# A GRU scan with a mixture of experts on one core: the order of TensorE's products by stationary width, and the update gate's place in PSUM

## What is computed

```
for each step:  gi = x_t @ W_ih + b_ih ;  gh = h @ W_hh + b_hh          # 512 -> 3*512
                r, z = sigmoid(i_r + h_r), sigmoid(i_z + h_z)
                n = tanh(i_n + r * h_n) ;  h = (1 - z) * n + z * h
tokens = all h:  logits = tokens/|tokens| @ router_w  -> softmax, top 2 of 8, renormalised
out = x + sum_e combine[:, e] * (tokens @ Wa[e] @ Wb[e])                 # 512 -> 128 -> 512
```

## Time and profile before

| what | value |
| --- | --- |
| time, median of 3 runs | 1042.74 us (1042.63 to 1043.17) |
| the profiled execution | 1042.57 us |
| its span | 1040.8 us |
| busy: TensorE, its weight loads, VectorE, ScalarE, GpSimd | 97%, 80%, 83%, 69%, 29% |
| mean granted clock of TensorE | 0.998 |

### The profile page before, as it was taken

How to read it: one execution, slowest core, us unless ns; L and a number is a source line. 1 busy time by engine, 2 the same in 40 slices (tenths; PEclk the granted TensorE clock), 3 DMA queues, 4 the chain that set the end, 5 groups by cost and what they waited for, 6 DMA issues and landing times.

```text
span 1040.8 us, 67010 instructions
## 1 busy us (share of the span) xinstructions
PE 1011.4 (97%) x28409; PEld 828.4 (80%) x28409; DVE 860.0 (83%) x3215; ACT 722.6 (69%) x2824; POOL 299.0 (29%) x762
## 2 busy tenths in 40 slices
PE   5789999999999999999999999999999999999997
PEld 3677888888888888888888888888888888888875
DVE  6889888888888888888888888888888888888886
ACT  7687666767666767667767667667766767766663
POOL 2032232322233332233332233332233332223223
PEclk9999999999999999999999999999999999999999
DMA  8230111111111111111111111111111011110001
GB/s 295 84 94 17 30 32 29 30 27 30 29 32 29 29 27 30 29 32 30 29 28 28 29 32 32 27 30 27 29 32 32 26 30 28 29 32 20 9 9 33
DMA packets 49522, 39.24 MB, mean 38 GB/s; under 512 B 34676, under 2 KB 39112, under 8 KB 49224
## 3 DMA queue, kind: packets, MB, share of 16 engines
q1 hardware_dynamic: 48376, 31.41, 11.1%
q10 hardware_dynamic: 848, 3.54, 1.0%
HBM read 18.94 MB, written 8.39 MB: 26 GB/s over the span
## 4 chain that ended last, share of the span: by engine, by line
PE 91%; DVE 5%; ACT 2%; DMA 1%; issue 1%; POOL 0%; ACTq 0%; DVEq 0%; POOLq 0%
PE ybank L1014 18%; PE pairs L883 17%; PE obank L1037 15%; PE gates L958 11%; PE gates L963 10%; PE nbank L912 7%; PE zbank L973 5%; PE zbank L969 5%; DVE tr L762 1%; PE nbank L994 1%; DMA wih<-in_L_cond_W_ih 1%; DVE pre L765 1%; DVE acc L815 1%; ACT nn L624 1%; DVE pre L771 1%
## 5 line engine op out<-in xcount | busy, mean ns | idle before, releaser
L883 PEld LDWEIGHTS pairs<-wx,xs 128*32 128x32 f16 x6144 | 140.7, 96 | 105.8 <-issue 101.7
L883 PE MATMUL pairs<-wx,xs 128*32 128x256 f16 x6144 | 215.6, 275 | 0.0
L1014 PE MATMUL ybank<-hparts,wa 128*128 128x128 f16 x3024 | 212.5, 220 | 0.0
L458 POOL TENSOR_TENSOR y<-y 128x128 f16<-128x128 f32 x256 | 111.7, 436 | 348.1 <-ACT y L658 190.0
L1037 PE MATMUL obank<-wb,y 128*128 128x512 f16 x738 | 199.3, 379 | 0.0
L1014 PEld LDWEIGHTS ybank<-hparts,wa 128*128 128x128 f16 x3024 | 169.8, 98 | 26.9
L762 DVE STREAM_TRANSPOSE tr<-gates 128x256 f32<-128x256 f32 x256 | 115.1, 450 | 72.4 <-PE gates L963 68.5
L616 ACT ACTIVATE rr<-pre 128x64 f32<-128x64 f32 x256 | 65.7, 257 | 155.6 <-DVE pre L765 155.2
L958 PE MATMUL gates<-whh,st 128*32 128x256 f16 x4080 | 155.8, 273 | 11.3 <-DVE st L788 10.8
L963 PE MATMUL gates<-whh,hparts 128*32 128x256 f16 x4080 | 155.9, 273 | 0.0
L815 DVE SCALAR_TENSOR_TENSOR acc<-obank,comb,acc 128x512 f32<-128x512 f32 x184 | 136.9, 744 | 0.2
(11 more groups left out here) (134 smaller groups left out, 1701.4 us busy)
## 6 DMA issues: line engine op xcount, KB each, us to landing
out<-outb SPq DMA_DIRECT2D x63, 128.0 KB
xin<-in_x SPq DMA_DIRECT2D x58, 128.0 KB
wih<-in_L_cond_W_ih ACTq DMA_DIRECT2D x4, 768.0 KB, 7.7
whh<-in_L_cond_W_hh SPq DMA_DIRECT2D x4, 768.0 KB, 11.8
wih<-in_L_ffn_Wb SPq DMA_DIRECT2D x8, 256.0 KB, 2.7
xs<-xh SPq DMA_TRANSPOSE x116, 2.8
wih<-in_L_ffn_Wa SPq DMA_DIRECT2D x4, 256.0 KB, 4.2
whh<-in_L_ffn_Wa SPq DMA_DIRECT2D x4, 256.0 KB, 2.6
```

Of the source, the lines that this page charges most:

```text
L458: nc.gpsimd.tensor_tensor(y[:, m % YB, 1, :], y32[:, :], y[:, m % YB, 0, :], ALU.subtract).then_inc(ylo_ready, 1)
L883: mm = nc.tensor.matmul(bank[32 * j:32 * j + 32, P:3 * P], turned(b, k, ph)[:, t0:t0 + 2 * B], wx[:, pw, k, j, :], start=False, stop=(k == ...
L1014: mm = nc.tensor.matmul(y_at(m)[:, 0:P], wa[:, pw, k, e, :], hparts[:, f % HB, k, :, ph * B:(ph + 1) * B], start=(n == 0), stop=(n == 3 * ...
```

## The change

Steps are now of two kinds. An odd step, behind its `state_part`, does only products with 128 stationary columns: the last term of the second expert's `expert_up`, an `expert_down`, all 12 products of an `n_part`, the route at s = 3, and a second `expert_down`. An even step does only products with 32 stationary columns, and it does a whole `pair_part` (48 products) and then five of the six terms of two experts' `expert_up`. A term there is four products in the four column groups, each with 32 of the 128 stationary columns and all 512 moving ones.

For that PSUM is dealt out anew. `zbank` is gone: the update gate of step n is in columns 256 to 383 of `gates[(n + 1) % 2]`, the bank in which the next step's other gates are made, so the products of the update gate also wait until `seed(n + 1)` is done. There are two output banks (`obanks`). The experts' middle is in `ybank` for even experts and beside the candidate's part in `nbank` for odd ones; the router's sums are beside it in `ybank`. On ScalarE `seed` now stands ahead of the router's copy and `split_y`. The expert work runs one step later (`DOWN`, `SPLIT` = 9, `ADD` = 14), so that 14 outputs, and not 13, are left behind the last step.

```
-    DOWN, UP, ADD = S, S + 5, S + 5
-    YB = UP - DOWN + 1
-    AHEAD = 3
+    DOWN, SPLIT, ADD = S + 1, S + 1, S + 6
+    YB = 6
...
-        zbank = ps("zbank", [P, 4 * P])
-        obank = ps("obank", [P, 4 * P])
+        obanks = [ps(f"obank{i}", [P, 4 * P]) for i in range(2)]
+        def z_at(n):
+            return gates[(n + 1) % 2][:, 2 * P:3 * P]
         def y_at(m):
+            return nbank[:, 2 * P:3 * P] if m % 2 else ybank[:, 0:P]
+        def router_at(f):
+            return (ybank if f < NB - 1 else gates[1])[:, P:P + NE + 1]
...
             def seed(n):
                 wait(act, rh_turned, n - 1)
+                wait(act, z_turned, n - 2)
...
             def add_gi_bias(b, m):
                 act.wait_ge(gi_done, K * b + m + 1)
-                if b >= 2 and m == 1:
-                    act.wait_ge(logits_done, b - 1)
+                if b >= 2:
+                    act.wait_ge(y_done, (b - 2) * NE + 2 * m + 2)
...
             def beside(n):                              # ScalarE
+                if n + 2 < T:
+                    seed(n + 2)
                 if s == 3 and 1 <= i:
                     read_router(i - 1)
-                if 0 <= n - DOWN:
-                    split_y(n - DOWN)
-                if n + 2 < T:
-                    seed(n + 2)
+                if 0 <= n - SPLIT:
+                    split_y(n - SPLIT)
...
                 mm.then_inc(rh_done, 1)
                 pe.wait_ge(z_seeded, n + 1)
+                pe.wait_ge(seeded, min(n + 2, T))
...
             def expert_down(m):
+                wait(pe, yhi_ready, m - 1)
+                wait(pe, y32_ready, m - 1)
+                if m % 2 == 0 and e >= NE // 2 and m < LAST:
+                    pe.wait_ge(router_read, f + 1)
+                if m % 2:
+                    pe.wait_ge(gi_ready, min(K * (f + 2) + m % NE // 2, K * NB))
...
+            def up_term(m, term, tiles):
+                ph, pw = TERMS[term]
+                rows = P // tiles
+                for j in range(tiles):
+                    mm = nc.tensor.matmul(o_at(m)[rows * j:rows * j + rows, :], y[:, m % YB, ph, rows * j:rows * j + rows],
+                                          wb[:, pw, m % NE, :], start=(term == 0), stop=(term == 2),
+                                          skip_group_check=True)
+                if term == 2:
+                    mm.then_inc(o_done, 1)
...
-            def beside(n):
-                i, s = n // S, n % S
-                if 0 <= n - DOWN < T:
-                    expert_down(n - DOWN)
-                if n == 1:
-                    n_part(1, 0, 0)
-                if 1 <= n and i + 1 < NB:
-                    n_part(i + 1, s // 2, s % 2)
-                if s == 3 and 1 <= i:
-                    route(i - 1)
-                if 0 <= n - UP < T:
-                    expert_up(n - UP)
-                if n + AHEAD < T:
-                    pair_part((n + AHEAD) // 2, (2, 3) if (n + 1) % 2 else (0, 1))
+            def beside_odd(n):
+                i, s = n // S, n % S
+                if 0 <= n - ADD:
+                    up_term(n - ADD, 2, 1)
+                if 0 <= n - DOWN:
+                    expert_down(n - DOWN)
+                if i + 1 < NB:
+                    n_part(i + 1, s // 2, n)
+                if s == 3 and 1 <= i:
+                    route(i - 1)
+                if 0 <= n - DOWN:
+                    expert_down(n - DOWN + 1)
+            def beside_even(n):
+                if n == 0:
+                    pair_part(1, (2, 3))
+                    turn_first(2)
+                elif n + 2 < T:
+                    pair_part(n // 2 + 1, range(K))
+                if 0 <= n - ADD:
+                    up_ready(n - ADD)
+                    for term in range(3):
+                        up_term(n - ADD, term, K)
+                    up_ready(n - ADD + 1)
+                    for term in range(2):
+                        up_term(n - ADD + 1, term, K)
```

More of the change, by code:

```diff
@@ L529, in last_experts @@
                     less_upper_half(NB - 1, part)
+                low_y(LAST - 1)
                 for m in range(LAST, T):
@@ L694, in last_experts @@
                     gather_states(NB - 1, part)
+                split_y(LAST - 1)
                 for m in range(LAST, T):
@@ L899, in put_first_biases, with n_part @@
                 mm.then_inc(bias_done, 1)
[L901 to L906, removed]
-                        pe.wait_ge(gi_ready, K * b + m)
-                    if b >= 2 and m == 2 and i == 0:
-                        pe.wait_ge(router_read, b - 1)
-                    mm = nc.tensor.matmul(n_at(b, m)[:, 0:P], win[:, pw, k, m, :], turned(b, k, ph),
-                                          start=(i == 0), stop=(i == 11), skip_group_check=True)
-                if half:
-                    mm.then_inc(gi_done, 1)
+            def n_part(b, m, n):
+                wait_turned(b)
+                pe.wait_ge(gi_ready, K * b + m)
+                wait(pe, yhi_ready, n - SPLIT)
+                wait(pe, y32_ready, n - SPLIT)
+                for k in range(K):
+                    for ph, pw in TERMS:
+                        mm = nc.tensor.matmul(n_at(b, m)[:, 0:P], win[:, pw, k, m, :], turned(b, k, ph),
+                                              start=(k == 0 and (ph, pw) == TERMS[0]),
+                                              stop=(k == K - 1 and (ph, pw) == TERMS[-1]), skip_group_check=True)
+                mm.then_inc(gi_done, 1)
             def first_parts(k):
@@ L944, in first_state_part @@
                             for j in range(K):
-                                mm = nc.tensor.matmul(bank[32 * j:32 * j + 32, 0:cols.stop - cols.start],
+                                mm = nc.tensor.matmul(bank[32 * j:32 * j + 32, :],
                                                       (st if pw else prior)[:, k, :], whh[:, pw, k, j, cols],
@@ L987, in route @@
                 for part in range(3):
-                    nc.tensor.matmul(nbank[:, P + NE:P + NE + 1], upper_half(part), ones_bf[:, :],
+                    nc.tensor.matmul(router_at(f)[:, NE:NE + 1], upper_half(part), ones_bf[:, :],
                                      start=(part == 0), stop=(part == 2), skip_group_check=True)
@@ L993, in route @@
                     for ph, pw in TERMS:
[L994 removed]
+                        mm = nc.tensor.matmul(router_at(f)[:, 0:NE], hf[:, ph, k, :], rw[:, pw, k, :], start=(n == 0),
                                               stop=(n == 3 * K - 1), skip_group_check=True)
@@ L1031, in expert_up @@
                     pe.wait_ge(rh_turned, T)
+                    pe.wait_ge(z_turned, T)
                 else:
                     pe.wait_ge(acc_done, m - len(last_o) + 1)
-                if m in wb_split_at:
-                    pe.wait_ge(weights_split, splits_before(wb_split_at[m]))
-                for n, (ph, pw) in enumerate(TERMS):
-                    mm = nc.tensor.matmul(o_at(m)[:, :], y[:, m % YB, ph, :], wb[:, pw, m % NE, :],
-                                          start=(n == 0), stop=(n == 2))
@@ L1067, in last_experts @@
                 for m in range(T + LEFT + 2 - LAST, T):
-                    expert_up(m)
+                    last_up(m)
             pe.wait_ge(consts_ready, N_CONST)
             zeros = st[:, :, :].rearrange("p k c -> p (k c)")
-            for g, n_cols in ((gates[0], 2), (gates[1], 2), (zbank, 1)):
-                for c in range(n_cols):
-                    mm = nc.tensor.matmul(g[:, c * P:(c + 1) * P], zeros, zeros, start=(c == 0), stop=(c == n_cols - 1),
+            for g in gates:
+                for c in range(3):
+                    mm = nc.tensor.matmul(g[:, c * P:(c + 1) * P], zeros, zeros, start=(c == 0), stop=(c == 2),
                                           skip_group_check=True)
```

85 lines of the change are left out of this document (44 added, 41 removed).

## The result

The changed kernel takes 1049.8 us (median of 4 executions, 1049.2 to 1050.8) against 1042.8: the ratio is 1.0067, 95% interval 1.0050 to 1.0085. It is slower, and the forecast of 1023 was wrong in sign.

The account below looks back on a forecast made before the run. TensorE's step (3.85 us) was taken as the bound, the state's loop (3.71) close behind. Blocks falling from 31.15 to 30.45 us save 20.0 over 28.5 blocks; the tail adds 0.9: 1042.6 becomes 1023, 8 in 10 within 1014 to 1036.

Parts of the forecast that it names:

- The loop of the state: Scan's second loop, from state to state: taken as 3.71 us, and 3.94 at s = 3 in the kernel before.
- TensorE's sums: TensorE's work per step after the change: even step 3.71 us, odd step 3.78, odd step with the route 4.16.
- the price of a change of mode: On TensorE between stationary operands of 32 and 128 columns: 0.11 us one way, 0.09 to 0.10 back; four become two.
- 4.16 at s = 3: TensorE's sum in us for the odd step that also holds the route, which adds 0.38 to 3.78.
- the seed being early enough for the update gate: ScalarE's seed ends 0.65 us behind the state, the update gate's products start at 1.02: covered by 0.37 us.
- The three rivals with a mechanism: Weight loads show (7 in 100), GpSimd's low part hits VectorE's addition (8), changes cost the same though fewer (4).
- The weight loads of the column groups: Rival, even steps: 20 narrow loads not hidden, 13.8 ns each or more, time 1052 or about 1082; 7 in 100.
- GpSimd's low part: Rival: GpSimd's low part of y delays VectorE's addition L765 by 0.23 us in all seven ordinary steps, 1062; 8 in 100.
- Nothing is asked of the issue that isn't done already.: TensorE's instruction issue: densest stretch now has a product every 13.8 ns, the new ones need one in 54.
- The 0.30 us in which the state lay ready: In an ordinary step of the kernel before, the state was done 0.30 us before TensorE turned to it.
- No more than that can be won in a step: TensorE's step of 3.85 us and the state's loop lie 0.14 us apart: that limits the gain, 32 us in 228 steps.
- The time in hand ahead of L765: GpSimd's L458 would end at 1.56 or up to 1.64, VectorE's L765 begin at 1.72: 0.1 to 0.17 us spare.

## Why the prediction was wrong

**What held.** The loop of the state and TensorE's sums were right to 0.02 us a block for the code as it stood. So were the price of a change of mode (0.12 and 0.08 for 0.11 and 0.10; the wide terms cost 0.2 for two), 0.216 for four column-group products at one time, 4.16 at s = 3, and the seed being early enough for the update gate. The three rivals with a mechanism are all out. The weight loads of the column groups are hidden: 1.08 for 20 products. GpSimd's low part doesn't hit L765: L780, its like in the kernel after, takes 0.29 outside s = 3, with 0.31 at s = 5 as the most (medians). From L777 to the state are 2.46 us in most steps as before, 2.50 and 2.52 at s = 4 and 5, and at s = 3 it is even 2.46, where 2.69 stood; the shift in time undid a clash. And the changes of mode that were removed are gone.

**The step that failed** is the one sentence on issue: "Nothing is asked of the issue that isn't done already." I compared the densest products (13.8 ns) with the new ones (54 ns), the rate within a stretch of half a microsecond. What runs short is counted over 256 instructions and over the sequencer's time, and both had changed:

- In an even step of 3.72 us there are 264 instructions of products and loads, in every step of the kernel before 218 in 3.85.
- There are 1432 waiting instructions and not 1057, at 106 ns of the sequencer each. I had costed waits only by whether what they wait for is late.
- The 0.30 us in which the state lay ready, which I booked as spare of the loop alone, was also the time in which the sequencer got past the head of `state_part` before TensorE was done with its old work. In both kernels the waiting instruction at that head starts 0.04 us behind the state; before, TensorE then still had some 0.25 us of old work, and with a loop that is tight it has none, and the densest stretches of the kernel follow.

Each of the three has a run that bears on it: taking away instructions (8 us), the other waits (24 us), or the wait at the head (26 us) brings back a third to all of the loss, and they don't add, since a piece that is in time can't be more so. The late steps fall from 22.2 us to 14.7, 1.5 and 6.3. Of the 26 us, and of the gain of each run without the wait at the head, some 5 are no late pieces but a shorter way from the state: the block's median falls from 30.47 to 30.28. For the third point the same wait was worth 1.3 us at the most in the kernel before, where the state lies ready. What is argued and not shown is the point at which the sequencer asks for a piece, and so why the place of a wait matters; I have only the lag, which orders the late steps well and not perfectly.

**Smaller terms.** The tail behind the last state takes 20.4 us where 19.0 stood, +1.4 for a predicted 0.85; step 20 begins 1.3 us later than before, with one break among the first steps, where I had put nothing. "No more than that can be won in a step" was too strict, as the bound of the loop held the time of a waiting instruction: in the last block, where TensorE waits for the state, its first product starts 0.15 us behind the state in the kernel before, and 0.05 where the wait rides on the weight load. So all even steps, the block's first too, go at TensorE's 3.72, the block's median is 30.28, and the time is 1018.2, below my 1023. The time in hand ahead of L765 was also off a little: 1.72 less 1.56 or 1.64 is 0.08 to 0.16 and not 0.1 to 0.17, which changed nothing. So the change itself is sound; it gives 2.4% once the waits that it made costly are gone.

## What to carry to other kernels

Where an engine's instructions go by as fast as here (256 in 3.3 to 3.6 us were too fast for a sequencer held up by waits, 256 in 4.07 were not), count the instructions per 256 and the waits between them, not only the work: a wait that another wait implies is not free, and one that stands ahead of a dense stretch on an engine that really waits there was the dearest here. When a run with added waits comes out slow, look at its granted clock before dividing. Let each instruction wait for one semaphore, the one that comes last in the other engine's order. Slack that a change uses up may have been hiding something besides the work that was seen in it.

## What the runs showed of the hardware

- TensorE's instructions arrive as pieces of 16384 bytes, one DMA of 0.9 to 1.5 us each in the kernels before and after (2.0 at the most in the other runs); the first product of a piece starts no sooner than 1.2 us after it has landed. Quieting 75% of the DMA packets changed neither.
- A waiting instruction takes 106 ns of TensorE's sequencer though its waits are long met (starts 0.106 us apart; three between two products put them 0.338 us apart), and has 51 ns in the profile. The run with 6400 more of them took 858 us longer, a part of which is the clock, granted at 0.805 on the mean.
- With one wait, on the weight load, the first product starts 0.05 us behind the state; a second makes an instruction of its own, and it starts 0.15 behind (last block of the kernel before, without and with it).
- Four products of 32 stationary columns and 512 moving ones in four column groups take 0.216 us, as one of 128 stationary columns does.
